# An opening re-ordered between engines, a pass's last sum on VectorE, and two blocks joined, in a graph network on one core

## The reference, cut to what matters

```python
x = x + _L0_gnn_ref(_layernorm(x), L0_gnn_W, src, dst, edge_weight)
x = x + _L0_ffn_ref(_layernorm(x)[None], ...)[0]      # attention, then 64 experts, top 2
x = x + _L1_gnn_ref(_layernorm(x), edge_index, ...)   # mean over neighbours, two products, batch norm
x = x + _L1_ffn_ref(_layernorm(x)[None], ...)[0]      # 8 experts, top 2
```

## Time and profile before

| what | value |
|---|---|
| median of 3 runs | 1431.85 us (1430.39 to 1435.46) |
| the profiled execution | 1431.99 us, of which span 1430.3 us |
| mean granted TensorE clock in it | 0.977 of full |
| busy: TensorE | 1364.4 us (95%) |
| busy: VectorE, ScalarE, GpSimd | 764.5, 454.3, 326.7 us |

### The profile page before, as it was taken

The page is one execution under the profiler, slowest core; times in us unless marked ns, Lnnn a source line. Parts: engine busy times, 40 slices in busy tenths (PEclk is TensorE's granted clock), DMA queues, the critical chain, the costliest instruction groups (busy, mean ns, idle before and its releaser), DMA issues. The chain is left out here.

```text
span 1430.3 us, 24305 instructions
## 1 busy us (share of the span) xinstructions
PE 1364.4 (95%) x7919; PEld 894.2 (63%) x7920; DVE 764.5 (53%) x1622; ACT 454.3 (32%) x1133; POOL 326.7 (23%) x489
## 2 busy tenths in 40 slices
PE   8999999999999999999998999999989999899994
PEld 4688864455457777777565777776545555656661
DVE  7899965572168888888465333333360011643336
ACT  2599950021045555555112111111350012211110
POOL 1388840000000000000122555555100000005540
PEclk9999999999999999999999999999999999879995
DMA  5000000040000000000513999999400000632226
GB/s 159 30 0 0 0 0 0 0 180 0 0 30 2 2 2 2 1 2 1 165 30 108 332 324 321 323 317 313 171 1 0 0 0 0 232 113 96 97 80 228
DMA packets 84196, 131.02 MB, mean 92 GB/s; under 512 B 11865, under 2 KB 49135, under 8 KB 83733
## 3 DMA queue, kind: packets, MB, share of 16 engines
q1 hardware_dynamic: 70303, 108.72, 23.1%
q0 software_dynamic: 12032, 18.17, 4.0%
q10 hardware_dynamic: 1788, 3.16, 0.8%
HBM read 115.33 MB, written 29.56 MB: 101 GB/s over the span
## 5 line engine op out<-in xcount | busy, mean ns | idle before, releaser
L1296 PEld LDWEIGHTS ps<-b_r 128*128 128x128 f32 x1024 | 124.3, 192 | 33.7 <-issue 32.2
L1200 POOL TENSOR_TENSOR b_x<-b_x,b_r 125x512 f32<-125x512 f32 x10 | 12.7, 1267 | 531.2 <-DVE b_r L1150 531.2
L1296 PE MATMUL ps<-b_r 128*128 128x78 f32 x1024 | 122.2, 273 | 1.2 <-DVE b_r L1373 1.2
L1305 PE MATMUL ps<-b_r 128*78 128x512 f32 x256 | 120.3, 593 | 0.0
L621 PE MATMUL ps<-b_r 125*125 125x160 f32 x660 | 117.6, 314 | 2.4 <-ACT b_r L534 2.4
L534 ACT ACTIVATE b_r<-b_r 125x125 f32<-125x125 f32 x330 | 108.2, 389 | 8.1 <-POOL b_r L340 3.7
L971 PEld LDWEIGHTS ps<-b_r 125*64 125x64 f32 x1600 | 85.3, 136 | 24.5 <-issue 22.8
L1356 ACT ACTIVATE b_r<-ps,b_r 128x78 f32<-128x78 f32 x128 | 34.6, 322 | 201.7 <-PE ps L1296 176.0
L934 PE MATMUL ps<-b_r 64*125 64x417 f32 (+1 forms) x480 | 94.8, 526 | 1.4 <-DVE ps L1063 1.2
L971 PE MATMUL ps<-b_r 125*64 125x125 f32 x1600 | 94.7, 272 | 1.3 <-ACT b_r L999 1.3
L621 PEld LDWEIGHTS ps<-b_r 125*125 125x125 f32 x660 | 92.0, 187 | 5.6 <-ACT b_r L534 3.9
(11 more groups left out here) (276 smaller groups left out, 2301.4 us busy)
## 6 DMA issues: line engine op xcount, KB each, us to landing
b_r<-L_ffn_w SPq DMA_DIRECT2D x128, 512.0 KB
b_r<-y SPq DMA_DIRECT2D x20, 512.0 KB, 7.4
b_r<-L_ffn_W SPq DMA_DIRECT2D x2, 4096.0 KB, 20.5
y<-b_r SPq DMA_DIRECT2D x2, 2500.0 KB
rows<-b_r SPq DMA_DIRECT2D x2, 2400.0 KB
b_x<-x SPq DMA_DIRECT2D x5, 480.0 KB
out<-b_x ACTq DMA_DIRECT2D x5, 480.0 KB
b_w_a<-L_gnn_W SPq DMA_DIRECT2D x2, 512.0 KB, 9.8
```

The costliest lines, as they stand in the source:

```text
L1296: last = pe.matmul(T.ps[:, 2 + r % 2, f * CAP:(f + 1) * CAP], T.ew1[r % WS][:, k, f * 128:(f + 1) * 128], T.ex_t[:, r % 2, k, :], start=(k ...
L1305: last = pe.matmul(T.ps[:CAP, 4 + r % 2, :], T.eh[:, r % 2, f, :], T.ew2[r % WS][:, f, :], start=(f == 0), stop=(f == FK - 1))
```

## The change

It does seven things.

1. The clears: VectorE clears `at[0:3000]`, GpSimd all the rest in four pieces; the last three wait until 2, 4 and 6 tiles are normalized. VectorE's two clears behind `prepare_edges` are gone.
2. The tile number `hi_f`: nine comparisons and additions become three instructions: subtract 62 and scale by 1/125, add `TO_WHOLE` (1.5 x 2^23, at which an f32 keeps whole numbers only), subtract it again.
3. ScalarE's order: the roots of tiles 6 to 9 are spread between copies, and the second table load is gone. `weighted_ready` and `weights_copied` are raised at the very start; so are TensorE's `counts_done` and `products_done`.
4. TensorE's order: `product(6)` goes ahead of `turn_edges`. `product(9)` writes bank 5 instead of bank 1, and so waits until the edge lists are out of that bank (`columns_ready`).
5. The tenth product is copied to SBUF after the pass; before it TensorE waits for nine copies, and for the tenth only ahead of the last of the ten matmuls that use it.
6. The last group's weights are added by VectorE straight from PSUM; ScalarE's last copy and GpSimd's last addition are gone.
7. `first_experts` and `second_convolution` become one block, so the barrier between them and the 12 filler products go. TensorE waits for `bias_added` instead.

```diff
-    link(dve.tensor_scalar(T.hi_f, T.src_f, float(P), None, ALU.is_ge))
-    for k in range(2, NT):
-        link(dve.scalar_tensor_tensor(out=T.hi_f, in0=T.src_f, scalar=float(k * P), in1=T.hi_f,
-                                      op0=ALU.is_ge, op1=ALU.add))
-
+    link(dve.tensor_scalar(T.hi_f, T.src_f, float(P // 2), 1.0 / P, ALU.subtract, ALU.mult))
+    link(dve.tensor_scalar(T.hi_f, T.hi_f, TO_WHOLE, None, ALU.add))
+    link(dve.tensor_scalar(T.hi_f, T.hi_f, TO_WHOLE, None, ALU.subtract))
...
-    BY_POOL, FIRST = 5000, 8000
+    BY_VECTOR, NEXT, LAST = 3000, 8000, 4500
...
+    def z_bank(t):
+        return t % 2 if t < NT - 1 else 5
...
-            pool.memset(at[:, 0:BY_POOL], 0.0).then_inc(S.sums_cleared, 1)
+            pool.memset(at[:, BY_VECTOR:NEXT], 0.0).then_inc(S.sums_cleared, 1)
+            for i, part in enumerate((at[:, NEXT:], ct[:, 0:LAST], ct[:, LAST:])):
+                pool.wait_ge(S.z_rows, 2 * i + 2)
+                pool.memset(part, 0.0).then_inc(S.sums_cleared, 1)
...
             def end_pass(seen):
-                for i in range(-3, 0):
+                for i in range(-3, -1):
                     sums, weights = add_weights(NG + i, (NG + i) % 2, seen, i)
                     pool.tensor_tensor(sums, sums, weights, ALU.add).then_inc(S.at_added, 1)
...
-            dve.memset(at[:, BY_POOL:FIRST], 0.0).then_inc(S.sums_cleared, 1)
+            dve.memset(at[:, 0:BY_VECTOR], 0.0).then_inc(S.sums_cleared, 1)
...
-            dve.memset(at[:, FIRST:], 0.0).then_inc(S.sums_cleared, 1)
-            dve.memset(ct, 0.0).then_inc(S.sums_cleared, 1)
             edge_columns(dve, link, T, S)
...
+                weights = window(dve, T.at, starts[1])
+                dve.wait_ge(S.products_done, seen + 2)
+                dve.wait_ge(S.at_added, seen + 2)
+                dve.tensor_tensor(weights, weights, products(3), ALU.add).then_inc(S.at_added, 1)
...
-            roots(3)
-            roots(4)
-            act.preload_act_table(ACT.Copy)
+            row_roots(act, T, S, 0, (6,))
             product_row(2)
             turned(2)
+            row_roots(act, T, S, 0, (7,))
+            roots(4)
             product_row(3)
...
             def last_weights(seen):
-                copy_weights(-1, seen)
...
+                act.wait_ge(S.at_added, seen + 3)
+                act.sem_inc(S.weights_copied, 1)
+
             act.wait_ge(S.columns_ready, 1)
             visits(act, "act", body, None, last_weights)
+            product_row(NT - 1)
...
             product(5)
+            product(6)
             turn_edges(pe, T, S)
-            product(6)
             turn(4)
-            for t in (7, 8, 9):
-                product(t)
+            product(7)
+            product(8)
+            pe.wait_ge(S.columns_ready, 1)
+            product(9)
...
-            pe.wait_ge(S.z_copied, NT)
-            pe.wait_ge(S.columns_ready, 1)
+            pe.wait_ge(S.z_copied, NT - 1)
             visits(pe, "pe", body, None, end_pass, peel=False)
...
+                    if t == 0 and k == NT - 1:
+                        pe.wait_ge(S.z_copied, NT)
...
-def second_convolution(nc, T, S, A):
...
-            keep_busy(pe, T, 7, 12)
+            pe.wait_ge(S.bias_added, NT)
             for t in range(NT):
...
+            dve.wait_ge(S.bias_added, NT)
```

114 lines of the change are left out of this document (53 added, 61 removed).

## The result

The changed kernel took 1421.01 us, median of four runs (1416.71 to 1421.6); the kernel before 1431.12, median of four as well (1430.0 to 1435.46). The ratio is 0.9916, 95% interval [0.9898, 0.9934]. Applied to the 1431.85 of before, that is 1419.8, between 1417.2 and 1422.4: faster, as forecast, but 3.4 us under the 1423.2 and 0.7 under the low end of 1420.5. The profiled execution took 1421.59, of which span 1419.9. Both pairs of medians are 10.1 us apart.

The account below looks back on a forecast made before the run. TensorE, busy 95% of the span, was taken as the bound. Gains of 5.4 (start of the pass), 0.8 (its end) and 2.6 (seam) sum to 8.8 us: 1431.99 becomes 1423.2, range 1420.5 to 1427.

Parts of the forecast that it names:

- The hole: Opening, TensorE between products 3 and 4: next turn at 30.54 instead of 34.70, 4.2 us (hole about 2.2, clock 1.9).
- Covers: Opening: edge lists ready at 33.2, needed from 38.3; VectorE in the pass at 46.2; product 9 covered by 4.8 us.
- The rival of clears that hold VectorE: Opening: VectorE stands for GpSimd's 9.1 us of clears, edge lists and pass come 4.0 late, 1427.2 at worst; chance 0.05.
- Start of the pass: First matmul of the pass at 51.6, 5.4 us earlier (4.9 to 6.0), with 0.55 of the 1.81 gap remaining.
- Pace of the pass: Inside the pass, after its first matmul: the same loop as before, so no gain was booked.
- End of the pass: From TensorE's last product to the next stage: one VectorE addition, next stage at 197.3, 0.8 us won (0.5 to 1.0).
- Seam: Between bias additions and first weighing: TensorE starts at about 1031.5 instead of 1034.09, 2.6 us won (2.3 to 2.8).
- The fourth rival: Late matmuls and second router: clock fall moves; sooner gives 1427.6 (chance 0.08), later or not at all 1418 (0.05).
- the rival's lucky half: Late stages: the clock's fall comes later or not at all, up to 5 us less, 1418; chance 0.05.
- The slower rival: Seam and weighing stage: without filler the clock falls, a tile takes about 3.6 us at half clock, 1437; chance 0.04.
- a clock below 1.00 behind the seam: Sign named beforehand: PEclk below 1.00 behind the seam would show the forecast wrong.

Follow-up runs that it names:

- the first attempt: Changed kernel, TensorE waiting for the turned weights' copies instead of the last bias addition before the first weighing: 1418.41 us; timed again, median 1421.48, ratio 0.9921.

## Why the forecast was right in direction and too small

**The hole (4.2): right.** The turn of the fourth pair starts at 30.35 instead of 34.70, and 0.16 of the 4.35 is the earlier start of product 3. ScalarE's order was the cause, and the clears and the order on TensorE its condition: the runs with ScalarE's order alone and with the clears back show both. The split into 2.2 for the hole and 1.9 for the clock is what the profiles of before have (more exactly 1.7, 5.39 less 3.70), but two of the five profiles with the old order lost none of the 1.9. That it stood in the profile that I read, and in the next, was luck.

**Covers (edits 1, 2, 4): right.** Lists turned from 38.07 (forecast 38.3), VectorE in the pass at 46.2 (46.2), nothing lost at product 9. The rival of clears that hold VectorE did not come: no row of VectorE is longer beside them. But those rows are statistics and small instructions; none with two inputs in SBUF and no large one-input copy or scaling met a clear, so whether a clear would hold such an instruction was not put to the test. "SBUF — State Buffer" of the Trainium skill, section "SBUF: two separate sides", locks a shared port pair against VectorE instructions with two inputs in SBUF only where GpSimd's also reads SBUF. The trace agrees for one that reads: GpSimd's matrix of 45.47 took 1.01 beside VectorE's L412 (45.52, two inputs in SBUF), and 0.60 at 51.35, beside VectorE instructions that have one input in PSUM.

**Start of the pass: the step that failed first.** "What remains of the 1.81 is the load and the loop's set-up: between 0 [...] and 1.1", of which I took the middle, 0.55. It is 0. The earlier trace rows had the load at 55.9, 0.7 behind the end of the products, and I read this as its own time; it was the wait for the copy, behind which the sequencer stood. A time at which an instruction starts says when it was let go, not that it couldn't have run before. From the start of the last products to the pass 1.97 us are won where 1.26 was forecast, since the pass also starts 0.16 ahead of the modelled end of the last product. With the 0.16 of product 3, the opening gives 6.3 instead of 5.4.

**Pace of the pass: the step that failed most.** "From there on the pass is the same loop" put this term at nothing. The loop is the same, but with three more instructions ahead of it in GpSimd's list each of the last eight borders of rounds costs 0.1 us less and one 0.3; 1.2 us are won inside the pass in all. No row of before could have told this.

**End of the pass (0.8): right,** 0.8. **Seam (2.6): right in kind,** 2.9: TensorE starts 0.05 behind the last addition, not 0.3.

Together 6.3 + 1.2 + 0.8 + 2.9 = 11.2 at the three places and inside the pass, where 8.8 was forecast. Both pairs of medians say 10.1, but their intervals reach from 9.5 to 14.6 and from 6.2 to 12.3 us, so they don't show that anything of the 11.2 is missing. If one us is, a part of it can be the fall behind the hole: where it is absent, as in two profiles of five, the opening is worth 1.7 less; by that share it would be 0.7 less on average, an estimate from five profiles.

**The clock's falls** elsewhere come and go, and I have no rule for them. The stop ahead of L832 (L844 in the changed file) is 0.90 or 0.91 us in all fifteen profiles, and the clock falls behind it in nine: in both of the changed kernel and in five of the seven of its variants, in neither of before and in two of the four of its variants. It falls in the variant with the clears back, where the stage starts at 288.18, and not in the one with the copy ahead, where it starts at 288.22. So neither the code nor an earlier start decides it; the 1.7 us lost there in the table can't be put down to the change. Both profiles of before have a fall at 770 to 775 (0.66), which the second of the changed kernel lacks. "TensorE: Matmul & The Clock Gate" of the Trainium skill, Part 1, lets the engine's recent activity decide. That like stops differ from run to run, as here, I could not forecast from rows of one execution.

**The fourth rival's places** moved too. In both profiles of the changed kernel the second router is shorter than in both of before (23.5 and 23.4 us against 28.0 and 26.6), and so are the last products, first to last start (12.0 and 11.8 against 13.8 and 12.4). That is the rival's lucky half, 4.5 and 1.8 us in the first pair of profiles, and part of why the first pair comes to 10.4 in spite of the 4.1 lost among the experts. But over all fifteen profiles the router takes 23.3 (the kernel before with the blocks joined) to 28.0, and the last products 11.8 to 14.4 with either kernel, so it isn't shown to be the change's.

**The slower rival** did not come: over the stage of the weighings the clock is 1.00 in the changed kernel, in the joined blocks alone and in the first attempt, with TensorE standing 1.13 and 0.4 between tiles. One sign that the prediction named did appear, a clock below 1.00 behind the seam: 0.72 from 1056 to 1062 in the first profile of the changed kernel, 28 us behind the first weighing. The second profile of before has the same behind its own stage (0.66 from 1064 to 1069), with barrier and filler in place, and the second of the changed kernel hasn't (1.00 from 1052 to 1060); so nothing ties it to the missing filler.

## What to carry to other kernels

A wait's price includes all that its engine's sequencer could have done meanwhile: before pricing what is left behind a removed wait, ask whether those steps need anything but the sequencer, and if not, expect them to cost nothing (here 1.1 us of load and set-up did). Fillers that keep a clock up belong where the engine stands anyway; behind a wait they are paid in full, 2.6 us here. When a hole is closed, follow every other engine to the new due time first, since a hole's neighbours (here VectorE's clears) can be just as late.

## What the runs showed that I had not expected

- Three more instructions in GpSimd's list ahead of a loop made the loop's border about 0.1 us cheaper eight times and 0.3 once, 1.0 us over eleven rounds, without any change to the loop.
- The same stop of TensorE may or may not lower its clock: 2.22 and 2.44 us did (next product 5.39), 2.43 in another kernel did not (3.70); the one of 0.90 ahead of L832 did not, the one of 0.91 ahead of L844 did. Each such fall, in these two places, cost 1.7 us.
- Stages with the same code take one of two or three lengths from run to run (the experts 236.1, 238.5 or 240.1 us from first to last start, the longer ones with a fall of the clock at their beginning; the last products from 11.8 to 14.4), more than most single edits here are worth. The timeline at the place of the edit shows a gain of 0.8 us; the median of six runs doesn't.
